# A state-space layer and a mixture of experts on one core: each g load as two row transfers, and the experts' outputs stored from ScalarE's queue

## What is computed

```python
# state-space branch (per batch, over time; 256 channels d, 64 states n)
dA = exp(dt[:, :, None] * A)
h  = dA * h + dt[:, :, None] * b[:, None, :] * xt[:, :, None]
y  = einsum('bdn,bn->bd', h, c)            # c repeats with a period of 64 steps
out1 = (y + x * D_param) @ out_proj_w.T
# feed-forward branch: 64 experts, the best 6 of each token, and a shared one
h = einsum('th,ehi->tei', x2d, w1_experts)
a = relu(h)**2 * route_w[:, :, None]
out2 = shared + einsum('tei,eih->th', a, w2_experts)
```

## Time and profile before

| | |
|---|---|
| median of 3 runs | 1863.0 us (1857.44 to 1863.48) |
| profiled execution | 1870.53 us, its span 1868.2 us |
| busy in the span | PE 1031.4 us (55%), DVE 932.9 (50%), ACT 577.6 (31%), POOL 573.8 (31%) |
| mean granted TensorE clock | 0.646 of full speed (its levels are 1.2 and 2.4 GHz) |
| DMA | 232.80 MB, mean 125 GB/s |

### The profile page before, as it was taken

The page is one execution under the profiler, slowest core; times in us unless marked ns, Lnnn a source line. Parts: engine busy times, 40 slices in busy tenths (PEclk is TensorE's granted clock), DMA queues, the critical chain, the costliest instruction groups (busy, mean ns, idle before and its releaser), DMA issues. The chain is left out here.

```text
span 1868.2 us, 21312 instructions
## 1 busy us (share of the span) xinstructions
PE 1031.4 (55%) x6823; PEld 572.8 (31%) x6824; DVE 932.9 (50%) x842; ACT 577.6 (31%) x847; POOL 573.8 (31%) x391
## 2 busy tenths in 40 slices
PE   3775056465564565645655555646656556554335
PEld 3443012233332343323333223323323233331114
DVE  5796899433342343433334233333334233348994
ACT  1124533333332333423333233323323233332210
POOL 2016770222222222223223223213222222226770
PEclk8898555566666666666666576666676566765557
DMA  9903831333333333333333343333343333335332
GB/s 340 304 0 110 284 116 35 103 124 108 121 122 96 121 125 115 116 106 124 121 113 101 108 128 121 121 97 124 105 128 119 102 119 120 113 122 153 103 101 93
DMA packets 187707, 232.80 MB, mean 125 GB/s; under 512 B 48201, under 2 KB 143818, under 8 KB 187338
## 3 DMA queue, kind: packets, MB, share of 16 engines
q1 hardware_dynamic: 178378, 206.12, 34.5%
q0 software_dynamic: 9216, 25.18, 4.3%
HBM read 154.05 MB, written 77.07 MB: 124 GB/s over the span
## 5 line engine op out<-in xcount | busy, mean ns | idle before, releaser
L969 DVE TENSOR_TENSOR_SCAN H<-ps,U 128x1024 f32<-128x1024 f32 x256 | 584.9, 2286 | 252.6 <-ACT ps L700 91.1
L601 POOL TENSOR_TENSOR U<-X,B 128x1024 f32<-128x1024 f32 x100 | 234.6, 2346 | 987.4 <-DMA X<-g_d 972.8
L1133 PE MATMUL ps<-PK,sel 24*128 24x512 bf16 x824 | 242.4, 583 | 267.7 <-DVE H L969 127.0
L700 ACT ACTIVATE ps<-ps,Acur 128x1024 f32<-128x1024 f32 x256 | 279.8, 1093 | 272.6 <-PE ps L1133 272.5
L953 DVE TENSOR_TENSOR U<-ps,B 128x512 f32<-128x512 f32 x98 | 67.5, 689 | 591.8 <-PE ps L1133 591.8
L1192 PE MATMUL ps<-ident,XG 128*128 128x128 f32 x360 | 98.1, 427 | 476.4 <-DMA XG<-xg_d 476.4
L1122 PE MATMUL ps<-H,CB 128*32 128x128 f32 x4096 | 269.9, 401 | 13.6 <-DVE H L969 6.1
L724 ACT COPY XT<-ps 128x512 f32<-128x512 f32 x90 | 52.7, 586 | 606.3 <-PE ps L1192 606.3
L1192 PEld LDWEIGHTS ps<-ident,XG 128*128 128x128 f32 x360 | 63.1, 213 | 518.4 <-issue 505.3
L1133 PEld LDWEIGHTS ps<-PK,sel 24*128 24x128 bf16 x824 | 44.4, 98 | 442.3 <-issue 280.2
L1181 PE MATMUL ps<-WE,AS 128*128 128x256 f32 x360 | 179.2, 650 | 0.0
(11 more groups left out here) (146 smaller groups left out, 593.5 us busy)
## 6 DMA issues: line engine op xcount, KB each, us to landing
X<-g_d SPq DMA_DIRECT2D x100, 512.0 KB
WE<-w_exp_dram SPq DMA_DIRECT2D x184, 256.0 KB, 6.3
xg_d<-CB SPq DMA_DIRECT2D x23, 1024.0 KB, 11.1
XG<-xg_d SPq DMA_DIRECT2D x92, 256.0 KB, 13.5
yg_d<-YO SPq DMA_DIRECT2D x90, 256.0 KB, 19.4
PK<-pk_d SPq DMA_DIRECT2D x64, 128.0 KB, 10.0
pk_d<-GS SPq DMA_DIRECT2D x16, 256.0 KB, 3.5
X<-x_dram SPq DMA_DIRECT2D x4, 512.0 KB, 5.6
```

The costliest lines, as they stand in the source:

```text
L601: nc.gpsimd.tensor_tensor(U[:, c % 4, :], rows, B2[:, b * L:(b + 1) * L], ALU.mult).then_inc(u_pool, 1)
L700: nc.scalar.activation(a_tile(c), a_tile(c), ACT.Exp, scale=Acur[:, b, pair:pair + 1]).then_inc(a_ready, 1)
L969: V.tensor_tensor_scan(H[:, (s // GRP % 2) * GRP + s % GRP, :], a_tile(s), U[:, s % 4, :], 0.0, ALU.mult, ALU.add).then_inc(scan_done, 1)
L1133: return mm(ps[:, bank, :], sel[32 * g:32 * g + ROWS, c % SUB, :], PK[32 * g:32 * g + ROWS, c // SUB % NPK, :], start=True, stop=True)
```

## The change

load_g issues two transfers in place of one: each reads one row of g_d, repeats it 64 times, and fills 64 of the slot's 128 partitions, the second channel's first. Each adds 16 to the slot's semaphore, so GpSimd waits for counts of 32 a load. The store of YO moves from SP's program to ScalarE's, with the same wait, at the same step; it stands behind the experts' copies of the step and ahead of the GS copy.

```diff
--- before.py
+++ after.py
@@ -417,9 +417,10 @@
             def load_g(block_no, c):
 
                 b, pair = c // PAIRS % NBATCH, c % PAIRS
-                sp.dma_start(gslot[dma_slot(c)],
-                             g_d[bass.ds(block_no * CH + 2 * pair, 2), b, :].unsqueeze(1).broadcast_to((2, N, L)))\
-                    .then_inc(s_gs[dma_slot(c)], 16)
+                for d2 in (1, 0):
+                    sp.dma_start(gslot[dma_slot(c)][d2 * N:(d2 + 1) * N, :],
+                                 g_d[bass.ds(block_no * CH + 2 * pair + d2, 1), b, :].broadcast_to((N, L)))\
+                        .then_inc(s_gs[dma_slot(c)], 16)
 
             for q in range(4):
                 h, b = q // 2, q % 2
@@ -499,12 +500,6 @@
                             m = (it - PRE) * MPI + j
                             sp.wait_ge(moe_L2, m + 1)
                             load_expert(m + 2, (j + 2) % MBUF)
-                        j = s // 2 - 2 if s % 2 == 0 else MPI - 1 if s == SL - 1 else -1
-                        if j >= 0:
-                            m = (it - PRE) * MPI + j
-                            sp.wait_ge(moe_out, m + 3)
-                            sp.dma_start(yg_d[bass.ds(m * 2 * P, 2 * P), :].rearrange("(u p) d -> p u d", p=P),
-                                         YO[:, j % MBUF, :, :]).then_inc(s_mo[j % MBUF], 16)
 
             for it in range(PRE):
                 body(it, False)
@@ -593,7 +588,7 @@
                     if not beyond(it, c) and on_gpsimd(it, c):
                         rows = gslot[dma_slot(c)] if g_rows_dma(it, c) else GS[:, act_slot(c), :]
                         if g_rows_dma(it, c):
-                            pool.wait_ge(s_gs[dma_slot(c)], (by_dma(it, c) - dma_slot(c)) * 16 // NGS + 16)
+                            pool.wait_ge(s_gs[dma_slot(c)], (by_dma(it, c) - dma_slot(c)) * 32 // NGS + 32)
                         else:
                             pool.wait_ge(g_copied, 2 * by_act(it, c) + 2)
                         pool.wait_ge(scan_done, it * SL + c - 3)
@@ -727,6 +722,12 @@
                         act.wait_ge(s_mo[(j - 1) % MBUF], (it - PRE) * (16 * MPI // MBUF) + (j - 1) // MBUF * 16 + 16)
                         nc.scalar.copy(YO[:, (j - 1) % MBUF, :, :].rearrange("p u d -> p (u d)"), ps[:, 6, :])\
                             .then_inc(moe_out, 1)
+                    j = s // 2 - 2 if s % 2 == 0 else MPI - 1 if s == SL - 1 else -1
+                    if moe and j >= 0:
+                        m = (it - PRE) * MPI + j
+                        act.wait_ge(moe_out, m + 3)
+                        act.dma_start(yg_d[bass.ds(m * 2 * P, 2 * P), :].rearrange("(u p) d -> p u d", p=P),
+                                      YO[:, j % MBUF, :, :]).then_inc(s_mo[j % MBUF], 16)
                     for k, c in copies(it, s):
                         act.wait_ge(g_bcast, g_counts(it, c, k)[0])
                         if k == 0 and not (isinstance(it, int) and it * SL + c - 8 < NPRE):
```

## The result

The changed kernel takes 1220.61 us (median of 4 runs, 1220.24 to 1222.3), the kernel before 1863.24. The ratio is 0.6558, its 95% interval 0.6544 to 0.6572. The prediction was 1200 us.

What follows compares the result with a forecast made beforehand. Two DMA engines carrying each g load were taken to bound the loop. Six blocks of 114.8 us instead of 222.6 save 647 us, plus 16 before the loop: 1863 - 663 = 1200 us, range 1125 to 1370.

Steps and rivals of the forecast that it cites:

- 10.0 + 3.9 us per pair: Loop: g load's 10.0 us plus other transfers' 3.9 on the same two DMA engines make the 13.9 us period.
- that SP is held: Loop: SP holds 4.5 us at the median to issue a YO store, because the two engines' rings are full.
- (c): g loads: the repeated row gives sixteen engines the same 52 GB/s, so no gain, 1863 us; chance 0.04.
- (d): g loads: both transfers land on one engine, 10 us more per pair, some 2820 us; chance 0.03.
- The 7.2 us: Loop: forecast length of a pair of steps, 6.65 from the fast stretch plus 0.15, 0.2 and 0.2.
- ScalarE's 0.2: Loop: the YO store's issue on ScalarE delays the GS copy, 0.2 us per pair, bounds 0 and 0.45.
- XG's 0.2: Loop: allowance for TensorE's leftover wait for the XG load, 0.2 us per pair.
- the clock's 0.15: Loop: TensorE's clock stays high once long XG waits go, with a few lapses, 0.15 us per pair.
- The jump's 1.5: End of each loop block: 1.5 us assumed for the jump, within the 114.8 us per block.
- (a): Loop: the DMA engines become the bound, pair 8.5 to 9.4 us, time 1317 to 1398 us; chance 0.17.
- (b): Loop: TensorE's clock stays low, pair 9.35 us, time 1394 us; chance 0.08.
- (e): YO store on ScalarE takes 4.5 us as on SP, 4.1 new, 387 us more, 1587 us; chance 0.02.

Runs made afterwards that it cites:

- e3: Kernel before, each g load made two transfers by halves of the time steps, each still from two rows: 1867.47 us, ratio 1.0018.
- e5: Changed kernel, but g stored in two copies and each g load one transfer from 4 source rows: 1418.0 us on a slower chip, ratio 0.7393.
- e4: Changed kernel, but g stored in eight copies and each g load one transfer from 16 source rows: 1249.62 us, ratio 0.6699.
- e2: Kernel before with only the YO store moved to ScalarE, g load still one transfer from two rows: 1857.56 us, ratio 0.9957.
- e8: Changed kernel with each g transfer bringing only the first 512 time steps: 1265.58 us on a slower chip, ratio 0.6616.
- e1: Changed kernel with the YO store back on SP, so the two row transfers alone: 1205.05 us, ratio 0.6466.
- e7: Changed kernel with g broadcast ahead of transposes, GS copy ahead of XT copy, store behind both: 1203.09 us on a slower chip, ratio 0.6285.
- e10: Changed kernel with the loop's six blocks written out on every engine: 1233.28 us on a slower chip, ratio 0.6438.
- e11: Same as e7 but with the YO store back on SP: 1233.22 us on a slower chip, ratio 0.645.
- e9: Changed kernel itself, unaltered, run again on a slower chip: 1271.22 us, ratio 0.664.

## Why the prediction was right

**The bound.** Two of the sixteen DMA engines, 10.0 + 3.9 us per pair: shown. e3, e5 and e4 set the number of engines by the source's outermost rows, and the loop follows the sum (13.9 us with two; 8.9 worked out with four and 143.0 us a block measured against 141). One side sign was read too broadly: that SP is held isn't the two engines' doing alone, but its own queue's behind the g loads (e2).

**The spread.** It came as expected, with shares of 0.12 to 0.14 in 4 windows of 697; rivals (c) and (d) are excluded. The price of a g load, put between 1.25 and 2.5 us of all engines, is 1.8 to 2.3 by the shares of the changed kernel and of e8. Two transfers serve no better than one with the same spread (e4). The Trainium skill (DMA: Bandwidth & Descriptors, Rules for kernel authors) advises against two transfers into halves of the partitions because both halves are spread over all sixteen engines anyway, and e4 agrees; the advice does not hold where the single transfer would use two engines, which the measured 0.6466 of e1 decides. The Trainium skill (DMA: Bandwidth & Descriptors, Why a DMA increments its semaphore by 16 and not by 1) takes the number of engines from the outermost dimensions, which gives 2, 16 and 4 for e3, e4 and e5, and the shares and loops of all three agree.

**What is late next.** TensorE's stream: shown by e7 and e8. The pair of the earlier trace rows was worth 6.65 us, without a store on ScalarE; the mean of the four lengths is 6.55 us without it (e1) and 6.75 with it. The lengths of single pairs differ by 0.9 us with their place in the block, and the prediction read one and compared it with no other: that it lay near the mean was luck.

**The terms of the pair.** The 7.2 us measured 7.00, the mean of the 84 intervals inside blocks. In place of 6.65 stand 6.55; ScalarE's 0.2 is 0.18 to 0.20 (e1); XG's 0.2 is nothing (4.4 us in the run); the clock's 0.15 is 0.25, what the mean has above the 6.75 at full clock. The few lapses that the prediction allowed for are more: the clock falls without long XG waits too, as in the pair at 628.92 us, 0.79 with TensorE busy 7.15 of 8.14 us. Two terms were too high, by 0.1 and 0.2 us, and one too low by 0.1.

**The end of a block.** The term that was mis-sized: 5.3 us for the pair without full expert work and 1.5 assumed for the jump, 6.8 in all. A block is 14 intervals between transposes and one of 18.0 us, which less a pair of 7.0 is 11.0. The 5.3 holds: written out (e10) the end is 12.18 us, which less a pair of 6.65 is 5.5. The jump's 1.5 does not: it stops TensorE for 5.0, and without it the end is 5.9 us shorter. My 1.5 came from no row. That this hid was luck: the pair was set too high, and 114.8 us were worked out for a block against a sixth of 696.8, 116.1.

**Where the 20 us went.** Predicted 663 us saved, measured 642.6. The loop saved 641.1 and not 647. Ahead of it 13.8 (block 1 starts at 342.01 in place of 355.84) and not 16. The last block grew by 5.3 us, where I had put nothing: 174.4 to 179.8 us between SP's load of its rates and the end. In the profile before, 26 scans and 23 products of 1024 were left for VectorE behind that mark; now 28 and 25 are, 7.0 us more of the engine that is busiest there. That VectorE had caught up ahead of the mark while the other engines were late is argued, not tried. The rows of the changed kernel:

```profile
L970 DVE TENSOR_TENSOR_SCAN H<-ps,U 128x1024 f32<-128x1024 f32 x28 | 63.9, 2282 | 0.2 <-ACT ps L695 0.2
...
L950 DVE TENSOR_TENSOR U<-ps,B 128x1024 f32<-128x1024 f32 x25 | 30.0, 1199 | 0.0
```

The remaining 7 us are the offset between profile and median: the profile before was 7.5 us above its median, which I took to be the same for both; the changed kernel's is 0.1 above.

**Rivals and signs.** (a) and (b) did not come: e8, and a clock of 0.91. (e) fell by e2, and its reason was wrong as well: ScalarE's issue isn't held when SP's is. (Its 4.1 us new to the forecast is the issue less 0.41; its 387 us go by 4.3, the issue less the 0.2 already in the sum.) Of the signs, all came but one. GpSimd still waits 79.4 us for X, not under 50. Little hangs on it: e8, which cuts this wait to 20.8 us, gains 4.8 us.

## What to carry to other kernels

When the DMA engines look one third busy and every load is late, look for short windows in which one load is alone: a share of 2/16 names both the transfer and the cure, and the outermost dimension of its source (here 2, against 128 partitions) is what to change, not the number of transfers. Before a large wait goes, read from the least hindered stretch of the trace what stands behind it, and from more than one pair; here it gave the pair within 2%. A place for a moved DMA issue is judged by what stands behind it on its engine, and the judgement can turn when the order around it gets faster (e1 and e11).

## What was not expected of the hardware

ScalarE's queue took a store in 0.38 us while SP's, on the same sixteen DMA engines and behind its own g loads, took 4.48 at the median.

A loop's jump stopped TensorE for 5.0 us. Written out, the loop was 40 us shorter, 29 of it at five block ends. The clock fell at a block's start in both, to 0.55 and 0.50 over the first pair of block 4, so the stop alone does not explain it.

Another chip ran the same kernel 50 us slower, all of it outside the loop. Block 1 started at 374.95 us in e9 and at 342.01 on the first chip. From 200 to 342 us, in the first part of which GpSimd issues indirect transfers, VectorE was busy 104.7 us in e9 and 133.0 on the first chip, and waits appear in e9 whose releaser the trace only calls remote:

```profile
ACT ps L695 <- remote: 36.4, 4, 10.1
...
DVE U L950 <- remote: 31.8, 5, 7.8
```

The stage after the loop, where GpSimd gathers, was 16 us longer. What it is stays open; no run tells, nor whether it is the chip.
